# Zeroing the strips outside the band for four heads in one selection, with the order of all work drawn anew

## The reference

```
B, S, _ = query.shape
q = _heads(query @ Wq.T + bq)
k = _heads(key @ Wk.T + bk)
v = _heads(value @ Wv.T + bv)
scores = jnp.einsum('bhqd,bhkd->bhqk', q, k) / np.sqrt(D_HEAD).astype(np.float32)
idx = jnp.arange(S)
local = jnp.abs(idx[:, None] - idx[None, :]) <= WINDOW // 2
scores = jnp.where(local[None, None, :, :], scores, -jnp.inf)
attn = jax.nn.softmax(scores, axis=-1)
ctx = jnp.einsum('bhqk,bhkd->bhqd', attn, v)
```

## Time and profile before

| | |
|---|---|
| median of 3 runs | 3426.66 us (3424.33 to 3450.11) |
| the profiled execution's own time | 3435.32 us |
| its span | 3433.6 us |
| PE busy | 3106.0 us (90%) |
| DVE busy | 2341.6 us (68%) |
| ACT busy | 1699.0 us (49%) |
| POOL busy | 1180.4 us (34%) |
| mean granted PE clock | 0.966 |

### The profile page before, as it was taken

One profiled execution on the slowest core, in us unless ns is written; L12 is line 12 of the kernel. 1 busy time (PEld: TensorE's weight loads), 2 busy tenths in 40 slices (PEclk: granted clock), 3 DMA queues, 4 the chain that ended last, 5 costly groups with the idle time before them and its releaser, 6 DMA issues.

```text
span 3433.6 us, 75982 instructions
## 1 busy us (share of the span) xinstructions
PE 3106.0 (90%) x29836; PEld 2298.5 (67%) x29836; DVE 2341.6 (68%) x5037; ACT 1699.0 (49%) x3496; POOL 1180.4 (34%) x1308
## 2 busy tenths in 40 slices
PE   7889989899999999999999999999989989889987
PEld 6766666676666666666676666667666657667764
DVE  5687567667686776768667686766757585543576
ACT  1245554454545555464555545455454534545545
POOL 7886006044151613416162341606234162100010
PEclk8899999999999999999999999999999989999999
DMA  7211001010111101011010101001011101000000
GB/s 224 69 56 32 20 20 50 17 57 20 39 29 29 41 17 54 20 35 29 26 47 20 49 25 36 28 26 47 20 42 32 38 23 53 11 1 1 11 26 11
DMA packets 123275, 122.77 MB, mean 36 GB/s; under 512 B 9776, under 2 KB 122672, under 8 KB 122800
## 3 DMA queue, kind: packets, MB, share of 16 engines
q1 hardware_dynamic: 122928, 117.91, 11.7%
HBM read 113.69 MB, written 4.19 MB: 34 GB/s over the span
## 4 chain that ended last, share of the span: by engine, by line
PE 62%; DVE 14%; POOL 10%; ACT 7%; issue 6%; DMA 1%; SPq 0%; DVEq 0%; POOLq 0%; ACTq 0%
PE banks L748 18%; PE banks L740 14%; PE banks L886 7%; PE banks L908 6%; PE banks L947 5%; DVE nmx L1260 5%; POOL work L1641 5%; ACT work L1491 4%; POOL work L1661 3%; PE banks L733 2%; PE banks L851 2%; POOL work L1651 2%; PE banks L954 2%; DVE added L1278 1%; PE banks L920 1%
## 5 line engine op out<-in xcount | busy, mean ns | idle before, releaser
L748 PE MATMUL banks<-work,weights 128*128 128x256 f32 x3584 | 849.7, 386 | 23.0 <-DVE work L1284 8.8
L748 PEld LDWEIGHTS banks<-work,weights 128*128 128x128 f32 x3584 | 665.4, 191 | 155.0 <-issue 33.4
L1491 ACT ACTIVATE work<-banks 128x1024 f32<-128x1024 f32 (+3 forms) x703 | 600.3, 908 | 295.6 <-PE banks L920 250.4
L1260 DVE TENSOR_REDUCE nmx<-banks 128x4 f32<-128x1024 f32 (+1 forms) x560 | 608.2, 1126 | 200.9 <-PE banks L886 199.7
L740 PE MATMUL banks<-weights,work 128*128 128x256 f32 x2688 | 664.5, 394 | 18.8 <-DVE work L1284 6.5
L740 PEld LDWEIGHTS banks<-weights,work 128*128 128x128 f32 x2688 | 505.2, 195 | 131.9 <-issue 42.4
L1651 POOL TENSOR_TENSOR work<-work 128x512 f32<-128x512 f32 x256 | 415.3, 1643 | 101.2 <-DVE work L1221 92.3
L886 PE MATMUL banks<-work 32*128 32x256 f32 (+1 forms) x5120 | 364.5, 400 | 82.8 <-DVE nmx L1260 29.2
L908 PE MATMUL banks<-work 32*128 32x256 f32 (+1 forms) x5120 | 372.6, 401 | 65.5 <-DVE nmx L1260 33.1
L1278 DVE TENSOR_TENSOR added<-work 128x1024 f32<-128x1024 f32 x192 | 270.0, 1406 | 183.2 <-ACT work L1491 157.0
L1641 POOL TENSOR_TENSOR work<-work 128x512 f32<-128x512 f32 x256 | 338.5, 1342 | 107.4 <-DVE work L1217 85.7
(11 more groups left out here) (160 smaller groups left out, 3627.9 us busy)
## 6 DMA issues: line engine op xcount, KB each, us to landing
weights<-in_w_all SPq DMA_DIRECT2D x322, 256.0 KB, 2.7
work<-in_w_setup SPq DMA_DIRECT2D x41, 256.0 KB, 5.8
work<-in_ctx SPq DMA_DIRECT2D x32, 256.0 KB, 3.0
work<-in_x SPq DMA_DIRECT2D x16, 256.0 KB, 3.0
out<-work SPq DMA_DIRECT2D x16, 256.0 KB, 2.2
weights<-in_w_all SPq DMA_DIRECT2D x1, 3072.0 KB, 14.9
row<-in_rows SPq DMA_DIRECT2D x1, 1280.0 KB, 9.2
mrow<-in_mask SPq DMA_DIRECT2D x16, 32.0 KB, 3.2
```

The lines of the kernel that those rows point to most:

```text
L748: ins = e.matmul(b[:, m * 256:m * 256 + 256], wslot(w)[:, k, m * P:m * P + P], xin[:, k, :], start=(k == 0 and (m == 0 or closed)) if star ...
L1260: ins = e.tensor_reduce(nmax(s, n)[:, 2 * p + j:2 * p + end, :], b.rearrange("p j (c n) -> p j c n", c=NC)[:, :, :, 0:w], AX, ALU.max, neg ...
L1491: ins = e.activation(dst, b.rearrange("p j (c n) -> p j c n", c=NC)[:, :, :, 0:w], ACT.Exp)
```

## The change

Three edits. The band step is one for a quad: it waits for both exponentials and then zeroes the strips of four heads with four selections, each over twice as many elements as before. In the list for the planner it is one step with an estimate of 1.9 us after both exponentials, where there were two of 1.0 us, each after its own exponential. And SEEDS has one number fewer in its middle and three more at its end, 24 in place of 23.

```diff
-SEEDS = (..., 207843, 86077, 805968, 561942, 32633, 126238, 798516, 91813, 237616, 902168)
+SEEDS = (..., 207843, 86077, 561942, 32633, 126238, 798516, 91813, 237616, 70655, 141016, 376773)
...
         if kind == "x":
-            e = [do("POOL", "band", (n, p), 1.0, e[p]) for p in range(2)]
+            e = [do("POOL", "band", n, 1.9, *e)]
         pv = do("PE", "pv", n, 1.3 if kind == "c" else 0.9, *e, *both, v,
...
                         if kind == "x" and kc == 0:
-                            e.wait_ge(*when("band", a, 0, i))
-                            e.wait_ge(*when("band", a, 1, i))
+                            e.wait_ge(*when("band", a, i))
...
                 elif op == "band":
-                    n, p = a
-                    e.wait_ge(*when("exp", n, p, i))
-                    both = pt(half_of.get((i, n), 0), 2 * p, 2)
+                    for p in range(2):
+                        e.wait_ge(*when("exp", a, p, i))
+                    heads = pt(half_of.get((i, a), 0), 0, 4)
                     for lo, hi, base, sign in ((0, WINDOW, WINDOW, 1), (WINDOW, SPAN, 0, -1), (256, 256 + P, 0, 1),
                                                (256 + P, 256 + SPAN, 0, -1)):
-                        part = both[:, :, lo:hi]
+                        part = heads[:, :, lo:hi]
                         ins = e.affine_select(out=part, in_=part, compare_op=ALU.is_ge, fill=0.0, base=base,
-                                              pattern=[[0, 2], [sign, hi - lo]], channel_multiplier=-sign)
-                    ins.then_inc(*tell(pool[s], "band", n, p, i))
+                                              pattern=[[0, 4], [sign, hi - lo]], channel_multiplier=-sign)
+                    ins.then_inc(*tell(pool[s], "band", a, i))
```

More of the change, by code:

```diff
@@ L71 @@
 RSLOT = {n: i for i, n in enumerate(ROWS)}
-SEEDS = (519167, 634534, 875864, 704644, 851259, 37516, 529412, 612800, 351972, 744357, 284174, 279811, 642892, 207843, 86077, 805968, 561942, 32633, 126238, 798516, 91813, 237616, 902168)
+SEEDS = (519167, 634534, 875864, 704644, 851259, 37516, 529412, 612800, 351972, 744357, 284174, 279811, 642892, 207843, 86077, 561942, 32633, 126238, 798516, 91813, 237616, 70655, 141016, 376773)
 SLOTS = 10
```

## The result

The changed kernel takes 3580.77 us (median of 4 runs, 3576.46 to 3598.99); the kernel before, run beside it, takes 3425.49 us (4 runs, 3411.14 to 3450.11). The ratio is 1.045 [1.041, 1.049]: 155 us slower. The forecast was 3421 us with a range of 3380 to 3465.

What follows compares the result with a forecast made beforehand. PE was taken as the bound, busy 3106.0 of 3433.6 us, its idle time being what counts. Selections -13, the new order's waits, array division and split exponentials summed to -6 us: 3426.66 - 6 = 3421 us, range 3380 to 3465.

Steps and rivals of the forecast that it cites:

- The rival in which most `pv` stand for the selections: Merged selections on POOL run late behind products, so `pv` on PE waits in most quads: 3482 us, chance 0.08.
- the one of the larger selections holding up DVE's sums: Longer POOL selections block DVE's sums at the shared SBUF ports: 15 us more, 3436 us, chance 0.05.
- The order by counts: For PE's waits, measured price of one times change in close places: -19, +5, +6, +5, +3, +8 us.
- `rs` behind `rs`: On PE, a second `rs` close behind the first, waiting for the causal mask: 11 places become 1, -19 us.
- `eq` behind `st`: On PE, `eq` close behind an `st`: 9 places become 27, one wait costs 0.51 us, taken as +5 us.
- `s` behind `cq`, `ck`: On PE, `s` close behind the cell's queries or keys: 28 places become 39, +6 us.
- `st` behind its `nm`: On PE, `st` right behind its `nm`: 7 places become 14, 6.4 us in 10 waits before, +5 us.
- `nm` behind its `s`: On PE, `nm` behind its `s`: fewer at one step or less, more at two or less; taken as +3 us.
- banks that `s` held: PE takes a bank that an `s` held at most one step earlier: 159 places become 179, +8 us.
- its weak point: Counts cover only pairs that made PE wait before; newly tight pairs have no row, only a 33 us allowance on idle time.
- The clock rival: PE idles in longer pieces, the granted clock in the middle falls from 0.98 to 0.96: 3473 us, chance 0.09.
- The signs to look for: Right: PE busy within 10 us of 3106, selection waits 10 us or less. Wrong: clock below 0.96, new wait over 20 us.

Runs made afterwards that it cites:

- the table of stalls above: PE's idle time ahead of each kind of step, kernel before against changed kernel: 249.9 to 342.9 us in the planner's simulated schedule, 327.6 to 415.5 us in the traces.
- the ten orders in the table: Kernel before, changed kernel and eight others with different SEEDS, split or merged step lists, listed by length of the planner's simulated schedule; 3405.6 to 3686.0 us.
- The four cases of old and new parts: Split or merged step list with old or new SEEDS: split old 3427 us, split new 3603, merged old 3686, merged new 3581.
- the first experiment: Kernel before with its order kept on every engine and only each quad's two band steps replaced by the merged one: 3423.02 us, ratio 0.9989 [0.9974, 1.0004].
- small products: POOL's linear-attention products cut to 2 of every 16 elements, nine memsets more: 3473.65 us in the changed kernel's order, 3327.24 us in the order of before.

## Why the prediction was wrong

**The merged selection was costed rightly.** Forecast: selections of about 420 and 640 ns, POOL busy near 1144 us, -13 us at PE. Measured: 425 and 647 ns, 1140.8 us, and a wait of 7.1 us over 4 times in place of 20.5. What this wait was worth in time is not shown: in the old order it fell by 9.4 us and the median by 4 us, inside the interval. The rival in which most `pv` stand for the selections did not occur. Nor did the one of the larger selections holding up DVE's sums, which take 1406 ns in the mean before, 1400 with the merged selections in the old order and 1384 in the kernel after.

**The order by counts was not.** Step by step, the wait of the pair before and after:

| pair | forecast us | measured us |
|---|---|---|
| `rs` behind `rs` (L1022 for L1338) | -19 | -16.2 (20.8 to 4.6) |
| `eq` behind `st` (L748 for L1491) | +5 | -1.7 (6.1 to 4.4) |
| `s` behind `cq`, `ck` (L886 for L1393) | +6 | -5.7 (16.3 to 10.6) |
| `st` behind its `nm` (L908 for L1475) | +5 | +9.0 (6.4 to 15.4) |
| `nm` behind its `s` (L896 for L1269) | +3 | +11.9 (18.1 to 30.0) |
| banks that `s` held (L908, L886 for L1260) | +8 | -13.2 (62.3 to 49.1) |

These six and the selections were forecast at -5 us together and measured at -29: the pairs that had a price came out better than forecast, and the kernel still lost. A count of places was a good guide only for `rs`, where the cause was one fixed pattern. For the others the wait per place was no constant: with more places for L1260 it fell by a fifth, and `nm` behind its `s`, which the two ways of counting put lower and higher, rose by two thirds. So a place decides little. That how late DVE or ACT runs at that moment decides more is likely, but was not measured.

**The step that failed** is the one that the text named as its weak point and then gave no price: pairs that the new order makes tight in ways that the old one never had. All the rows together fell by about 29 us while PE's idle time rose by 88. By the column of the trace in the table of stalls above, most of the rise lies before `st` of the cell (32.6 to 64.8 us), the transposes for the causal attention (0.1 to 27.3), the state's products (0.2 to 18.0), `s` of the last attention (7.2 to 24.2) and the cell's values (4.1 to 15.9). The text gave this "a tenth more or less", 33 us; it was 27%. It treated the idle time of the order as a fixed stock from which known rows are taken. The idle time of the ten orders in the table runs from 317 to 474 us, so the old one's 328 was near the low end of what lists of numbers give, and an order drawn anew should have been expected to lose. The four cases of old and new parts show it: the new numbers alone cost 176 us and the merged step list alone 259. The planner's own play, which needs no run, had most of these stalls and 93 us more idle PE. The sum also put a change of PE's busy time at nothing: it was to stay within 10 us of 3106 and rose by 59.

**The clock rival was partly right.** It had the middle fall to 0.96 and the time rise to 3473. The middle fell to 0.95 and PE's busy time rose by 59 us for the same 29836 records. By the mean granted clock, PE ran at the lower of its two levels (1.2 GHz in place of 2.4) for 2 x (1 - 0.966) x 3433.6 = 233 us before and 2 x (1 - 0.948) x 3580.8 = 372 us after, 139 us more. In the trace of the kernel after the products of L748 take 634 ns in the median in stretches at the lower level and 379 ns at the upper one. An estimate from these figures: at half the speed and with PE busy for 88% of the time, 139 us more at the lower level cost 139 x 0.5 x 0.88 = 61 us, near the 59 measured. The text kept this rival apart from the order. They go together: in the table the clock falls with PE's idle time, with small inversions, from 0.975 at 317 us to 0.941 at 474 us, whatever step list the order has. So with each microsecond of stall this kernel lost 1 + 59/88 = 1.7. That the stalls lower the clock, and nothing else that differs between the orders, is argued from these ten kernels; no run changed the idle time alone. The Trainium skill (TensorE: Matmul & The Clock Gate, Part 1) has an idle array throttled and released by activity; by that rule an order with more stalls pays twice, and the ten kernels of the table agree with it.

**The signs to look for** were set well in the main. L733 for L1200, 40 us longer, comes near "a new row over 20 us that has no counterpart", though it had one of 15.6 us that the rows did not show, and L1008 for L1319 is new with 18.0 us; "a granted clock below 0.96" is 0.948; and the sentence that a move of over 1% would be PE's idle time and not the merged selection is what the first experiment shows.

**What stays open.** That an order with a shorter play makes a faster kernel rests on ten cases, four of them forecast. The slope of 1.4 is made up of two parts: from the first row of the table to the last the play grows by 196, PE's idle time by 158 us and its busy time by 111, together 1.4 for each unit. For the changed kernel alone it is 147 us for 87, 1.7, and why it lies above the line is not known. What makes DVE late at L1319, whose stall the play has too, was not followed step by step. And small products give about 100 us in both orders, from which PE has 41 and 52 us less of busy time and 69 less of idle time; how that divides between POOL's results coming earlier and DVE's 112 us was not tried.

## What to carry to other kernels

An order that a search has found belongs to the step list and the estimates that it was found for. When a step changes, edit it within the finished order first, which isolates what it is worth (here nothing that can be told from noise), and when searching again, go on until the planner's own play is at least as short as the old one. A new list of numbers with a play 87 longer gave away 155 us. It did not even beat no list at all: with SEEDS empty the merged step list's play ends at 3370.9, the changed kernel's at 3399.3 (the empty list was played, not run on the chip). In costing a reordering, do not count only the pairs that wait now: compare a quantity that sums over all pairs, such as the play's length or PE's idle time in it step by step, and add what such idle time went with in the clock here.

## What the runs showed of the hardware

- **More idle time went with a lower clock.** From 317 to 474 us of PE idle time in a kernel that is 87 to 91% busy, the mean granted clock went, with small inversions, from 0.975 to 0.941 and PE's busy time for 29836 records from 3079.9 to 3190.5 us.
- **A DVE instruction with two SBUF inputs can take more than three times as long beside POOL's products**: L1190, 128x256, 475 to 486 ns in the old order, where no product overlaps it, 1081 to 1733 in the 14 instances of the new one that overlap a product, and 607 at most in the new order with small products.
- **POOL is busy for a third of the span and yet its products cost 100 us.** With 1/8 of the elements the old order took 3327 us in place of 3431. DVE's busy time fell from 2341.6 to 2229.1 us, though no instruction of DVE was changed; its sums L1278 are among what became shorter (1406 ns to these 1266, groups of DVE with each shape apart, old order with small products):

```profile
L1278 DVE TENSOR_TENSOR added<-work 128x1024 f32<-128x1024 f32 x192 | 243.0, 1266 | 189.2 <-ACT work L1491 160.7 <-issue 27.3
```
